# Two-layer cross attention: ScalarE's exponential of the image scores one slot later in its order

## The reference, cut to what matters

```python
probs_t = softmax(q @ k_t.T * attn_scale)
text_out = probs_t @ v_t
qsem = l2norm(probs_t @ text_ehs)
fused = q @ k_ip.T * attn_scale + 0.5 * (qsem @ l2norm(ip_ehs).T)
probs_ip = softmax(fused) * spatial_mask        # over 4 image tokens
out = (text_out + probs_ip @ v_ip) @ W_out + b_out + residual
```

## Time and profile before

| | us |
|---|---|
| median of 3 runs | 821.95 |
| the three runs | 822.62, 821.95, 817.98 |
| the profiled execution | 818.06 |
| its span | 816.3 |

### The profile page before, as it was taken

How to read it: one execution, slowest core, us unless ns; L and a number is a source line. 1 busy time by engine, 2 the same in 40 slices (tenths; PEclk the granted TensorE clock), 3 DMA queues, 4 the chain that set the end, 5 groups by cost and what they waited for, 6 DMA issues and landing times.

```text
span 816.3 us, 17251 instructions
## 1 busy us (share of the span) xinstructions
PE 780.0 (96%) x6392; PEld 634.3 (78%) x6392; DVE 562.7 (69%) x1539; ACT 425.4 (52%) x911; POOL 402.3 (49%) x297
## 2 busy tenths in 40 slices
PE   5979999999999999999999999999999999988796
PEld 5977778788888878787877788787887888766574
DVE  5447445757575767667858778788697797687745
ACT  5234624554546474647465465565555655555551
POOL 6421202201202040403658976887779768779763
PEclk9989989999999999999999999999999999999999
DMA  8874632946546564636353345254172342400010
GB/s 275 220 208 139 185 110 66 240 127 175 143 132 175 177 160 114 166 112 164 108 121 113 94 113 163 63 120 149 35 186 83 87 120 65 137 1 16 21 33 17
DMA packets 103027, 100.67 MB, mean 123 GB/s; under 512 B 10264, under 2 KB 102176, under 8 KB 102944
## 3 DMA queue, kind: packets, MB, share of 16 engines
q1 hardware_dynamic: 101408, 98.26, 43.7%
q10 hardware_dynamic: 1536, 1.31, 0.5%
HBM read 61.65 MB, written 36.74 MB: 121 GB/s over the span
## 4 chain that ended last, share of the span: by engine, by line
PE 75%; DVE 7%; issue 4%; SPq 4%; DMA 3%; ACT 3%; POOL 3%; POOLq 0%; DVEq 0%; ACTq 0%
PE pB L379 21%; PE pB L495 13%; PE pB L458 8%; PE pB L481 7%; PE pB L579 5%; PE pPV L522 4%; PE pPV L517 4%; PE pPV L527 4%; PE pB L536 3%; PE pPV L513 2%; POOL Y L1280 2%; DVE m_sb L1041 2%; DMA KP<-k0d 1%; DMA q1d<-qlo 1%; ACT P L842 1%
## 5 line engine op out<-in xcount | busy, mean ns | idle before, releaser
L1280 POOL TENSOR_TENSOR Y<-P,wv 128x512 f32<-128x512 f32 x120 | 156.3, 1319 | 109.2 <-ACT P L842 109.0
L1056 DVE TENSOR_TENSOR Y<-pB,Y 128x512 f32<-128x512 f32 x160 | 108.8, 685 | 68.9 <-PE pB L495 59.2
L458 PE MATMUL pB<-KP,QP 96*128 96x256 f32 x640 | 130.5, 289 | 4.5 <-DMA KP<-k0d 2.1
L458 PEld LDWEIGHTS pB<-KP,QP 96*128 96x128 f32 x640 | 107.1, 192 | 18.7 <-issue 7.3
L1257 POOL TENSOR_TENSOR klo<-xin,khi 128x256 fp32r<-128x256 f32 x18 | 13.2, 757 | 215.2 <-ACT khi L753 215.2
L1041 DVE TENSOR_REDUCE m_sb<-pB 128x2 f32<-128x504 f32 x160 | 107.9, 675 | 11.5 <-PE pB L458 9.8
L481 PE MATMUL pB<-QP,KP 100*128 100x512 f32 x320 | 109.4, 422 | 3.2 <-DMA QP<-mlo 2.7
L842 ACT ACTIVATE P<-pB 128x512 f32<-128x512 f32 x160 | 86.5, 596 | 44.8 <-PE pB L481 34.9
L842 ACT ACTIVATE P<-pB,ln 128x512 f32<-128x512 f32 x160 | 101.3, 692 | 0.0
L832 ACT ACTIVATE wv<-pB 128x512 fp32r<-128x512 f32 x120 | 66.8, 591 | 55.2 <-PE pB L481 53.9
L753 ACT ACTIVATE Vs<-pPV 128x512 f32<-128x512 f32 (+1 forms) x80 | 39.4, 492 | 100.8 <-PE pPV L517 67.5
(11 more groups left out here) (176 smaller groups left out, 1714.3 us busy)
## 6 DMA issues: line engine op xcount, KB each, us to landing
QP<-q0d SPq DMA_DIRECT2D x64, 192.0 KB, 4.1
KP<-k0d SPq DMA_DIRECT2D x64, 192.0 KB, 4.3
c_sb<-in_cT SPq DMA_DIRECT2D x16, 512.0 KB, 5.1
q0d<-qhi SPq DMA_DIRECT2D x32, 256.0 KB, 2.5
k0d<-khi SPq DMA_DIRECT2D x30, 256.0 KB, 2.5
q0d<-qlo SPq DMA_DIRECT2D x16, 256.0 KB, 2.8
k0d<-klo SPq DMA_DIRECT2D x15, 256.0 KB, 2.8
VB<-vipd SPq DMA_DIRECT2D x6, 640.0 KB, 4.0
```

Of the source, the lines that this page charges most:

```text
L458: made = mm(bank[:, sc * S:sc * S + S], QP[i][0:KROWS, j, a, sc * 128:sc * 128 + 128], KP[i][0:KROWS, j, :], start=True, stop=True)
L1056: tt(Y[:, p, dst, :], bank_of["gp", q, dst][:, :], Y[:, p, dst, :], MUL).then_inc(dv_y, 1)
L1280: tt(Y[:, p, ch, :], P[:, p, ch, :], PH[q % HR][ch].bitcast(F32), SUB).then_inc(po_y, 1)
```

## The change

ScalarE takes its part of the image softmax from the step `shares` instead of `soft`:

```diff
@@ scalar_program, main loop
                         elif what == "ot":
                             attention_back(*a)
-                        elif what == "soft":
+                        elif what == "soft" and not (True):
+                            image_weights(*a)
+                        elif what == "shares" and True:
                             image_weights(*a)
```

## The result

The changed kernel takes 829.17 us (median of 6 runs, 824.87 to 830.53), the kernel before 819.54 us (6 runs, 817.98 to 822.62). The two medians by themselves lie 9.6 us, 1.2%, apart. The forecast was 821.2 us within 816.0 to 825.5, and 0.78 for no change beyond 0.5%. It was wrong: the time lies above the range, on the side that had been given 0.10. The profiled execution of the changed kernel took 824.87 us, 6.8 us more than that of before, and was the fastest of its six. One execution of a later kernel (1248.32 us, at a mean granted clock of 0.56, of the gated kernel with the weights in slot 2) is left out of the ratios, which compare undisturbed executions.

A forecast was written before the change was run, and what follows sets the result against it. TensorE was taken to bound units 10 to 13, with no single bound in units 14 and 15. Terms -0.5 + 0 + 1.7 + 0 = +1.2 us gave 819.3 (profiled) or 823.2 (median), middle 821.2 us, range 816 to 825.5.

The forecast's parts named there:

- Units 10 to 13, 0: Four full rounds: TensorE idles only 0.14 us in each and GpSimd's subtractions just miss `soft`, so 0 us.
- Cover of the moved exponential: Unit 11 and the others: `ex` is done before VectorE asks for it, with over 3 us to spare in unit 11.
- third rival: ScalarE reaches `ex` early in units 14 and 15 and only waits at the new place: 0 us, 822; chance 0.2.
- Unit 14, +1.7 us: Unit 14: two GpSimd subtractions hold two VectorE lines, 1.9 us, less 0.2 back; shares and end come 1.7 us later.
- Unit 9, -0.5 us, at most +1.1: Unit 9: TensorE keeps most of its 0.83 us wait for `P`, VectorE is held at most 1.9: -0.5 us.
- Unit 15, 0, at most +1.5 us: Unit 15: VectorE's lines 1099 and 1103 held, +1.5 us, its 1.01 us wait gone, TensorE's transposes in time: 0.
- The sum and the median: Whole kernel: the places sum to +1.2 us, 819.3 from the profiled execution, 823.2 from the median; middle 821.2 us.
- fast rival: Units 9, 14, 15: TensorE's 6.5 us of waits and 3.3 us of lost clock return, 812 us; chance 0.2 with softer form.
- slow rival: Units 10 to 13: the holding of VectorE spreads to all rounds, +6.8 us in all, 828.7 us; chance 0.08.
- softer form: Units 9, 14, 15: VectorE not held at all, -4 us, about 818; chance 0.2 together with the fast rival.
- The range: Whole kernel: lower bounds sum to -4.8, upper to +5.5; from 821.2 and with run spread, 816 to 825.5 us.

The follow-up runs named there:

- gated kernel: Changed kernel, with GpSimd's slot 2 subtractions, and unit 9's output-weight ones, waiting until VectorE's `soft` chain is done; 0.9947 and, run again, 0.9980 of the kernel before.
- gated kernel with the weights in slot 2: The gated kernel with unit 9's output-weight rounding and subtractions moved from slot 1 to slot 2, without the gate on the weights; 0.9970 of the kernel before.
- 0.9997 by themselves: Kernel before with the image exponential moved only in units 10 to 13; 0.9997 of the kernel before.
- unit 14 alone: Kernel before with only unit 14's image exponential moved; 1.0020 of the kernel before.
- unit 9 alone: Kernel before with only unit 9's image exponential moved; 1.0036 of the kernel before.
- 128 partitions: GpSimd's second output-weight subtraction on 128 partitions instead of 64, in the changed kernel (1.0039 of the kernel before) and in unit 9 alone (one execution, 818.54 us).
- unit 15 alone: Kernel before with only unit 15's image exponential moved; 1.0020 of the kernel before.

## Why the prediction was wrong, by its own steps

- *Units 10 to 13, 0.* Right: -0.03 us in the trace, 0.9997 by themselves.
- *Cover of the moved exponential.* Right in substance: VectorE nowhere waits for `ex` in units 9 to 15. ScalarE's own wait was to fall under 10 us, with none left in unit 9; it fell to 13.3, because the held chain made it wait 4.15 us there. The third rival had this much right: in units 14 and 15 ScalarE does wait at the new place (3.19 and 3.21 us). Its 0 us was wrong.
- *Unit 14, +1.7 us.* Right, mechanism and size: the shares come 1.72 us later against the chain's first line, the stretch is 2.24 us longer in the changed kernel and 1.72 with unit 14 alone. That the delay reaches the end through GpSimd's chain was argued from the rows and has no experiment of its own. TensorE waits behind line 536 instead of before it, 2.41 us for 2.52.
- *Unit 9, -0.5 us, at most +1.1.* This step failed, and with it the sum. The forecast had the overlap with the weights' subtractions, but took each hold as the rest of one GpSimd instruction, 0.95 us. The first took 1.57 us and the second 3.36 for 0.33 each, 4.3 us of hold where at most 1.9 stood; the second lasted through three instructions. The stretch cost +2.65 us, and +4.02 in the trace with unit 9 alone, whose holds are the same and whose mean granted clock is 0.91 where the changed kernel's is 0.96. I also let TensorE "keep most of the 0.83", when the banks that it needs next are freed by the VectorE that is held; it then waited 2.17 us, and at 0.57 of its clock afterwards. The long hold needs the half-width instruction with subtractions ready behind it, which no row of before could show. Without it (128 partitions) unit 9 came out at -0.32 and -0.29 us, near the -0.5 forecast.
- *Unit 15, 0, at most +1.5 us.* The chain is as forecast: from line 1097 to the end of line 1105 it is 5.36 us, against 3.80 before, +1.56 for +1.5. TensorE's transposes were not late, either. This step failed by what it put at nothing. The forecast had no term for the clock: it removed one wait and looked only at whether the next instruction is in time, but the wait of 2.27 us moved right in front of TensorE's matmuls, and the low clock from ahead of line 561 to behind it. In front of line 561 the changed kernel is 0.65 us shorter, behind it 2.63 longer, about as much as the clock lost there; together +1.98. With unit 15 alone it was +1.25, and the gated kernel's two executions show that 1.5 us of such a stretch can be there or not. What sets whether the clock falls behind this wait isn't settled.
- *The sum and the median.* The three places give +6.9 us in the profiled execution (2.65 + 2.24 + 1.98, and nothing elsewhere), for 1.2 forecast. The timed ratio is 0.96% of 819.54, 7.9 us, with an interval of 6.1 to 9.6.
- *The rivals.* The fast rival, TensorE's 6.5 us coming back, needed that nothing be held: with the gate the gain is 0.2 to 0.5%, far from its 812 us and near its softer form of 818 (817.05 and 817.78). The slow rival had the right sign and the wrong place: the holds grew longer in unit 9, and did not spread to the full rounds. That its 828.7 us lie within 0.5 of the measured 829.17 is luck.
- *The range* added bounds place by place, and in unit 9 the bound was two holds of 0.95 us each, what the trace before happened to show. It was also formed unevenly: bounds of -4.8 and +5.5 are counted from no change, 820.0 in the forecast's own terms, which gives 815.2 to 825.5, and not from 821.2. The measured time lies above either.

## What to carry to other kernels

An engine that stands idle behind a wait may be keeping another one off a shared resource. Before its wait is taken away, list what its work releases and what that will lie on top of; here it was GpSimd's subtractions on VectorE's chain of additions between tiles in SBUF. If the earlier order is wanted all the same, gate the idle engine explicitly: waits at two places of GpSimd's program turned +0.96% into -0.2 to -0.5%. And where TensorE's wait is only moved, look at what it stands in front of.

## What the runs showed of the hardware

- A VectorE operation on 128x160 with both inputs in SBUF that starts beside a running GpSimd subtraction ends 0.18 or 0.19 us after that subtraction. Smaller ones are held as well, and end sooner behind it: line 1087 of the changed kernel, on 128x8, took 1.13 us in unit 15 (764.69 to 765.82, with the subtraction from 764.52 to 765.80) and 0.17 where no subtraction ran. A reduction is not held (line 1103, 0.32 us at 441.97 inside the subtraction from 441.72 to 443.09). In a row of GpSimd instructions the waiting one usually gets in between two of them, and the next GpSimd instruction then takes about 0.08 us longer (1.37 for 1.29). The Trainium skill (SBUF — State Buffer, "Who interferes with whom") states that of two such instructions one fully blocks, and that a reduction never contends. The 1.3 us of the held lines and the 0.32 us of line 1103 agree with it.
- Behind a GpSimd instruction on 64 partitions, with two subtractions ready behind it, the waiting VectorE operation was not let in at the following two boundaries: 3.36 us in two traces. With 128 partitions it was, 0.89 and 0.88 us in two traces. With 64 partitions and no subtraction ready behind it, it took 0.90 us in one trace. Why is open.
- After a wait of TensorE of 2.30 us the granted clock stayed at 1.00 in one execution of a kernel and fell to 0.71 over 4 us in another of the same kernel.
